# A decoder layer on one core: exponentials per PSUM bank, turned products alternating with scores, and the mixer's values in the ring banks

## The reference, cut to what matters

```python
x = x + mixer(layernorm(x))        # projection w1, depthwise conv, silu, running products
                                   # and sums over the tokens, C_w, D_w, gate w2, w3
x = x + attention(layernorm(x), ctx, ctx)
x = x + experts(layernorm(x))      # 8 experts, best 2, capacity 641, FF 1024
# attention: q from x; k, v from ctx; 16 heads of 16
scores = einsum('bhqd,bhkd->bhqk', q, k) * SCALE
scores = where(causal, scores, -inf)
probs = softmax(scores, axis=-1)
out = einsum('bhqk,bhkd->bhqd', probs, v) @ WO + bO
```

## Time and profile before

| | us |
|---|---|
| median of 3 runs (lowest to highest) | 697.65 (695.46 to 701.62) |
| the profiled execution's own time | 699.12 |
| its span, first to last instruction | 697.4 |
| mean granted clock of PE, as a share of 2.4 GHz | 0.926 |
| PE busy | 608.8 |

### The profile page before, as it was taken

How to read it: one execution, slowest core, us unless ns; L and a number is a source line. 1 busy time by engine, 2 the same in 40 slices (tenths; PEclk the granted TensorE clock), 3 DMA queues, 4 the chain that set the end, 5 groups by cost and what they waited for, 6 DMA issues and landing times.

```text
span 697.4 us, 11909 instructions
## 1 busy us (share of the span) xinstructions
PE 608.8 (87%) x4100; PEld 506.9 (73%) x4100; DVE 498.6 (71%) x1066; ACT 352.9 (51%) x685; POOL 334.2 (48%) x322
## 2 busy tenths in 40 slices
PE   3787998998989789899998725999999999999992
PEld 2666887787877545555564425999999999999991
DVE  6887687787688867678874442778787888788740
ACT  4774563663552333363534213566666666656551
POOL 1065324324340013331535464446776868686776
PEclk9897999999999989999987655999999999999997
DMA  8302306765338745955735006223626262621224
GB/s 281 119 31 43 109 31 160 258 180 150 92 93 226 170 112 139 240 147 155 191 117 184 23 15 199 99 86 91 163 41 179 27 178 30 172 32 14 26 33 45
DMA packets 63317, 81.65 MB, mean 117 GB/s; under 512 B 10296, under 2 KB 47939, under 8 KB 63257
## 3 DMA queue, kind: packets, MB, share of 16 engines
q1 hardware_dynamic: 53928, 72.85, 36.8%
q0 software_dynamic: 9216, 7.81, 7.8%
q10 hardware_dynamic: 112, 0.23, 0.1%
HBM read 48.27 MB, written 34.36 MB: 118 GB/s over the span
## 4 chain that ended last, share of the span: by engine, by line
PE 42%; DVE 5%; issue 4%; POOL 4%; DMA 4%; ACT 3%; ACTq 0%; SPq 0%; DVEq 0%; POOLq 0%
PE l_scores L101 13%; PE l_turned L1900 7%; PE l_out L1900 3%; PE l_shared L1900 3%; PE l_turned L340 2%; POOL out L1604 2%; ACT l_area L370 2%; PE l_scores L1834 2%; PE l_turned L324 2%; PE l_out L360 2%; PE l_shared L1776 2%; DMA l_q_more<-md 1%; PE l_scores L1857 1%; DMA l_hi<-md 1%; PE l_scores L265 1%
## 5 line engine op out<-in xcount | busy, mean ns | idle before, releaser
L2089 DVE SCALAR_TENSOR_TENSOR w_v<-w_th,l_scores 128x324 f32<-128x324 f32 x128 | 62.2, 490 | 55.0 <-ACT w_th L1691 53.7
L1691 ACT ACTIVATE w_th<-l_scores 128x324 f32<-128x324 f32 x128 | 56.4, 441 | 83.4 <-PE l_scores L101 82.1
L1591 POOL TENSOR_TENSOR l_lo<-w_v,l_hi 128x324 fp32r<-128x324 f32 x64 | 59.0, 922 | 74.6 <-ACT l_hi L1697 74.4
L370 ACT ACTIVATE l_area<-l_turned 128x1024 f32<-128x1024 f32 x48 | 49.1, 1023 | 82.4 <-PE l_turned L340 79.6
L101 PE MATMUL l_scores<-l_hi,w_w1h 128*128 128x324 f32 x256 | 81.0, 316 | 2.3 <-DVE l_lo L2081 1.2
L1604 POOL DMA_INDIRECT out<-l_area,w_to x48 | 76.3, 1591 | 12.0 <-issue 9.7
L101 PE MATMUL l_scores<-l_lo,w_w1h 128*128 128x324 f32 x256 | 80.3, 314 | 0.0
L101 PE MATMUL l_scores<-l_hi,w_w1l 128*128 128x324 f32 x256 | 80.1, 313 | 0.0
L294 DVE TENSOR_REDUCE l_nm<-l_scores 128x4 f32<-128x1024 f32 (+1 forms) x45 | 54.7, 1215 | 19.8 <-PE l_scores L280 19.6
L1697 ACT ACTIVATE l_hi<-w_v 128x324 fp32r<-128x324 f32 x128 | 59.9, 472 | 12.4 <-DVE w_v L2089 11.8
L2063 DVE TENSOR_TENSOR w_w2l<-w_s,w_w2h 128x256 fp32r<-128x256 f32 x56 | 60.9, 1088 | 1.9
(11 more groups left out here) (459 smaller groups left out, 1715.4 us busy)
## 6 DMA issues: line engine op xcount, KB each, us to landing
w_s<-in_L_ffn_w SPq DMA_DIRECT2D x14, 1024.0 KB, 7.4
disp<-c_blank SPq DMA_DIRECT2D x8, 658.1 KB
l_lo<-kd SPq DMA_DIRECT2D x26, 200.0 KB
l_hi<-qd SPq DMA_DIRECT2D x26, 192.0 KB
w_rows<-disp SPq DMA_DIRECT2D x7, 658.1 KB
kd<-l_qkh SPq DMA_DIRECT2D x16, 256.0 KB, 4.7
vd<-l_area SPq DMA_DIRECT2D x4, 1024.0 KB, 6.5
qd<-l_qkh SPq DMA_DIRECT2D x16, 256.0 KB, 4.2
```

The source lines that it names most:

```text
L370: act.activation(lead.pr[n % 3][:, :], lead.tbank[:, :], ACT.Exp, scale=SCALE).then_inc(A["exp"], 1)
L1591: pool.tensor_tensor(hl[:, g % 3, half(1)], v[:, n % 4, :], hh[:, g % 3, half(1)].bitcast(F32), ALU.subtract)\
L1691: act.activation(th[:, n % 2, :], hb[n % 2][:, 0:HALF], ACT.Tanh, scale=0.5).then_inc(F["th"], 1)
L2089: dve.scalar_tensor_tensor(v[:, n % 4, :], th[:, n % 2, :], 1.0, hb[n % 2][:, 0:HALF], ALU.add, ALU.mult).then_inc(F["v"], 1)
```

## The change

**Exponentials.** `exps` makes two ACT calls of 128x512, one per bank (e = 0, 1); `st` and `exp` are counted per bank, so every count that is compared with them doubles.

**Order of the products.** Where a step has both (t = 4 to 41), `turned_and_scores` takes the place of the separate parts: both masks of u; then for e = 0 and 1: the turned mask of that bank, which waits for the previous exponential of that bank alone, and the turned products of e alternating with the scores of 1 - e. Where one kind has four and the other two, the sequence is for example turned, score, score, turned, score, score. What the due steps put between turned products and scores (`ranks`) comes behind both.

**Mixer's values.** `V` leaves `PAIRS` (ten names, so each product keeps its pair in all blocks) and `values` writes ring banks 0 and 1. It waits for `ring` (chunk `A` 3 read) in place of `x_out` and `dx`; `mixed` waits for `x_out` and `dx` in place of `kl`; `turn_q` and `turn_x` wait for `kl` in place of `vf`; chunks `dl` 0 and `A` 0 of the next block wait for `vf`.

```diff
--- before.py
+++ after.py
@@ -164,7 +164,7 @@
 HIGH_ORDER = ("w1", "dl_w", "A_w", "B_w", "D_w", "WQ", "w2")
 LOW_VECTOR = ("w1", "dl_w", "A_w", "B_w", "D_w")
 LOW_GPSIMD = ("WQ", "w2")
-PAIRS = ("Q", "T", "D", "W1", "W2", "TC", "W3", "K", "V", "C", "TQ")
+PAIRS = ("Q", "T", "D", "W1", "W2", "TC", "W3", "K", "C", "TQ")
 LEAD = 6
@@ -212,7 +212,7 @@
 def lay(sp, A, M, lead, qd, kd, g):
     b, k = divmod(g, 2)
-    ge(sp, A["st"], 3 * (g - ITEMS + 1))
+    ge(sp, A["st"], 6 * (g - ITEMS + 1))
     if g == 0:
         sp.wait_ge(M["made"], 12 * NBLK)
         sp.wait_ge(M["D"], DC * NBLK)
@@ -266,19 +266,30 @@
                   start=True, stop=False, skip_group_check=True)
-def scores(pe, A, lead, u):
+def score(pe, lead, u, j, e):
+    g, s = divmod(u, 3)
+    p = j if s == 0 else 2 * s - 2 + j
+    rows, keys = slice(64 * e, 64 * e + 3 * HD), P if s == 0 else L
+    tok = slice(0, P) if s == 0 else slice(P, L)
+    at = e * 4 * P + j * keys
+    return pe.matmul(score_bank(lead, u)[:, at:at + keys], lead.q3[g % ITEMS][rows, p, tok],
+                     lead.k3[g % ITEMS][rows, p, 0:keys], start=False, stop=True, skip_group_check=True)
+def laid(pe, A, u):
     g, s = divmod(u, 3)
     if s == 0:
         pe.wait_ge(A[f"laid{g % ITEMS}"], LAID * (g // ITEMS + 1))
...
+def scores(pe, A, lead, u):
+    laid(pe, A, u)
+    for j in range(4 if u % 3 == 0 else 2):
+        for e in range(2):
+            mm = score(pe, lead, u, j, e)
     mm.then_inc(A["s"], 1)
@@ -307,46 +318,75 @@
     dve.transpose(lead.mt[g % 2][:, :], mx[:, :, :].rearrange("q n c -> q (n c)").bitcast(F32)).then_inc(A["mx"], 1)
...
+def turned_mask(pe, A, c, lead, n, e):
+    ge(pe, A["exp"], 2 * n + e - 1)
     if n == 0:
         pe.wait_ge(A["nm"], LEAD)
...
+    bank = lead.tbank[:, e * 4 * P:(e + 1) * 4 * P]
+    m = 4 if n % 3 == 2 else 2
+    out = bank.rearrange("k (p q) -> k p q", p=m)[:, :, 0:P]
+    pe.matmul(out, c["mask"][:, :], c["identb"][:, :].unsqueeze(1).to_broadcast([P, m, P]),
+              start=True, stop=False, skip_group_check=True)
+def turn_score(pe, lead, n, j, e):
+    g, s = divmod(n, 3)
+    p = j if s == 2 else 2 * s + j
+    rows = slice(64 * e, 64 * e + 3 * HD + 2)
+    tok = slice(P, L) if s == 2 else slice(0, L)
+    key = slice(P, L) if s == 2 else slice(0, P)
+    w = P if s == 2 else L
+    at = e * 4 * P + j * w
+    return pe.matmul(lead.tbank[:, at:at + w], lead.k3[g % ITEMS][rows, p, key], lead.q3[g % ITEMS][rows, p, tok],
+                     start=False, stop=True, skip_group_check=True)
+def maxima_in(pe, A, n):
     g, s = divmod(n, 3)
     if s == 0:
         pe.wait_ge(A[f"m_in{g % 2}"], 32 * (g // 2 + 1))
...
+def turned(pe, A, c, lead, n):
+    for e in range(2):
+        turned_mask(pe, A, c, lead, n, e)
+    maxima_in(pe, A, n)
+    count = 4 if n % 3 == 2 else 2
+    for j in range(count):
+        for e in range(2):
+            mm = turn_score(pe, lead, n, j, e)
+            if j == count - 1:
+                mm.then_inc(A["st"], 1)
+def turned_and_scores(pe, A, c, lead, t, u):
+    mask(pe, A, c, lead, u)
+    four_t, four_u = t % 3 == 2, u % 3 == 0
+    for e in range(2):
+        turned_mask(pe, A, c, lead, t, e)
+        if e == 0:
+            maxima_in(pe, A, t)
+            laid(pe, A, u)
+        for i in range(4):
+            if four_t or i % 2 == 0:
+                mt = turn_score(pe, lead, t, i if four_t else i // 2, e)
+                if i == (3 if four_t else 2):
+                    mt.then_inc(A["st"], 1)
+            if four_u or i % 2 == 0:
+                ms = score(pe, lead, u, i if four_u else i // 2, 1 - e)
+    ms.then_inc(A["s"], 1)
 def weigh(pe, A, lead, n):
     g, s = divmod(n, 3)
     b, k = divmod(g, 2)
-    pe.wait_ge(A["exp"], n + 1)
+    pe.wait_ge(A["exp"], 2 * n + 2)
     if s == 0:
         ge(pe, A["po"], 2 * g - 1)
         pe.wait_ge(A[f"v_in{b % 2}"], 16 * (b // 2 + 1))
@@ -365,9 +405,11 @@
 def exps(act, A, lead, n):
-    act.wait_ge(A["st"], n + 1)
     ge(act, A["pv"], n - 2)
-    act.activation(lead.pr[n % 3][:, :], lead.tbank[:, :], ACT.Exp, scale=SCALE).then_inc(A["exp"], 1)
+    for e in range(2):
+        act.wait_ge(A["st"], 2 * n + e + 1)
+        bank = slice(e * 4 * P, (e + 1) * 4 * P)
+        act.activation(lead.pr[n % 3][:, bank], lead.tbank[:, bank], ACT.Exp, scale=SCALE).then_inc(A["exp"], 1)
 def mixer_and_projections(nc, sems, c, lead, x_sb, bo, a, disp, qd, kd, vd, md):
@@ -851,7 +893,7 @@
                     if i == 0:
                         pe.wait_ge(S["ident"], 1)
                     ge(pe, S["xl2"], DC * (i - 2))
-                    ge(pe, S["vf"], 2 * (i - 1))
+                    ge(pe, S["kl"], DC * (i - 1))
                     turn([pair(i - 1, "T", k) for k in range(DC)], xn, "xT", ("xn", TPB * i))
                 def turn_c(i):
@@ -861,7 +903,7 @@
                     turn([pair(i, "TC", k) for k in range(DC)], cin, "cT")
                 def turn_q(i):
-                    pe.wait_ge(S["vf"], 2 * upto(i + 2))
+                    pe.wait_ge(S["kl"], DC * upto(i + 2))
                     turn([pair(i + 1, "TQ", k) for k in range(DC)], xn, "qT", ("xn2", TPB * i))
                 def products(name, m, xs):
@@ -882,6 +924,8 @@
                     if i == 0 and name == "B" and m == 0:
                         split_done(pe, "B_w")
                     ge(pe, S["ring"], made(i, name, m) - 4)
+                    if name in ("dl", "A") and m == 0:
+                        ge(pe, S["vf"], 2 * (i - 1) + (1 if name == "dl" else 2))
                     split_product(pe, ring(name, m)[:, :], products(name + "_w", m, (sh, sl))).then_inc(S["made"], 1)
                 def first_chunks():
@@ -914,7 +958,8 @@
                 def mixed(i, m):
                     pe.wait_ge(S["gh"], HC * (i + 1))
                     pe.wait_ge(S["gl"], HC * (i + 1))
-                    pe.wait_ge(S["kl"], DC * (i + 1))
+                    pe.wait_ge(S["dx"], DC * (i + 1))
+                    ge(pe, S["x_out"], 2 * i)
                     split_product(pe, pair(i, "C", m)[:, :], products("C_w", m, (gh, gl))).then_inc(S["C"], 1)
                 def w2(i):
@@ -923,9 +968,7 @@
                     pe.wait_ge(S["ssmh"], DC * (i + 1))
                     pe.wait_ge(S["ssml"], DC * (i + 1))
                     pe.wait_ge(S["dx"], DC * upto(i + 2))
-                    if i == NBLK - 1:
-                        pe.wait_ge(S["vf"], 2 * NBLK)
-                    else:
+                    if i < NBLK - 1:
                         ge(pe, S["ql"], DC * i)
                     for m in range(DC):
                         split_product(pe, pair(i + 1, "W2", m)[:, :], products("w2", m, late_input(i))).then_inc(S["w2"], 1)
@@ -962,12 +1005,11 @@
                         split_product(pe, pair(i, "K", m)[:, :], products("WK", m, (xbh, xbl))).then_inc(S["k"], 1)
                 def values(i):
-                    ge(pe, S["x_out"], 2 * i)
-                    pe.wait_ge(S["dx"], DC * (i + 1))
+                    pe.wait_ge(S["ring"], made(i, "A", 3))
                     for n in range(2):
                         for j in range(2):
                             tok = slice((2 * n + j) * P, (2 * n + j + 1) * P)
-                            mm = split_product(pe, pair(i, "V", n)[:, j * D:(j + 1) * D],
+                            mm = split_product(pe, banks[n][:, j * D:(j + 1) * D],
                                                [((xbh[:, k, tok], xbl[:, k, tok]), weights("WV", k, 0, D)) for k in range(DC)])
                         mm.then_inc(S["v"], 1)
@@ -982,14 +1024,14 @@
                 def unit(u):
                     if u == 0:
                         pe.wait_ge(S["ring"], 12 * NBLK)
+                        pe.wait_ge(S["vf"], 2 * NBLK)
                     if u == 1:
                         pe.wait_ge(S["hs"], DC * NBLK)
                     mask(pe, A, c, lead, u)
                     scores(pe, A, lead, u)
                 def step(t):
-                    turned_mask(pe, A, c, lead, t)
-                    turned(pe, A, lead, t)
+                    turned(pe, A, c, lead, t)
                 turn_x(0)
                 w1(0)
@@ -1209,7 +1251,7 @@
                         dve.wait_ge(S["vzero"], 1)
                     ge(dve, S["v_st"], 16 * i)
                     for s in range(2):
-                        ins = dve.tensor_tensor(v_rows(n, s), v_heads(pair(i, "V", n), s), v_heads(bv, s), ALU.add)
+                        ins = dve.tensor_tensor(v_rows(n, s), v_heads(banks[n], s), v_heads(bv, s), ALU.add)
                     ins.then_inc(S["vf"], 1)
                 dve.wait_ge(S["x0"], 16)
@@ -1904,17 +1946,13 @@
                 for t in range(START, END):
                     u = t + LEAD
-                    if t < NS:
-                        turned_mask(pe, A, c, lead, t)
                     if u < NS:
-                        mask(pe, A, c, lead, u)
-                    if t < NS:
-                        turned(pe, A, lead, t)
```

(20 more changed lines are left out.)

18 lines of the change are left out of this document (removed).

## The result

The changed kernel is slower. The forecast was 702.0 with a range of 689 to 710, so it is missed, upwards. The profiled execution took 715.32 us (span 713.6), 16.2 more than the one before.

The account below looks back on a forecast made before the run. PE was taken to bound mixer and attention. Profiled 699.1 plus attention 10.0 (13.5 - 6.6 + 3.1) less mixer 5.6 gave 703.5, or 702.0 us against the median; range 689 to 710, the forecast's own range 696 to 707.

Parts of the forecast that it names:

- The step that failed: Bound of mixer and attention: PE sets the time, so its work and stalls count; clock 0.95 read, no term given.
- three signs: Would refute the forecast: step with s = 1 at 1.9 us or less, lone products 0.2 apart, mixer under 3 us earlier.
- The longer steps: Attention: added PE work, less stalls removed, plus longer waits for the maxima, +10.0 us in sum.
- The passage: Attention, 38 steps: one more switch between full-height masks and half-height products, 0.29 us a step.
- The lone products: Attention, 25 steps with s = 0 or 2: unpaired half-height products take whole places, net 0.10 us a step.
- The third rival: Attention: a lone product can't load its weights ahead, 11 us on top, 713; chance 0.09.
- The stalls: Attention: 21 steps where the turned mask waits 0.31 us on average for the exponential; all go, -6.6 us.
- The maxima's way: Attention: maxima's transfers get 0.62 us less time, five groups without slack, +3.1 us.
- The mixer: Mixer blocks: values no longer wait for the residual, until DVE is late next; -5.6 us, between -2.5 and -7.5.
- The second: Attention: the maxima's transfers set the period and light groups wait 1.5 to 2 us, 708; chance 0.13.
- the first: Attention: alternation nearly free, passages 0.09 us a step, no tighter maxima transfers; -8.8 us, about 689; chance 0.22.
- the fourth: Mixer: none of the gain arrives because DVE's chain is the bound, 707.6; chance 0.08.

Follow-up runs that it names:

- passage_in_pairs: no_alternation with the scores' masks moved from ahead of the turned products to behind them, so a mask stands mid-step without alternation; 708.35 us, 1.018 of before.
- double_masks: Changed kernel with each turned mask multiplied twice in steps 4 to 41; 723.37 us, 1.037 of before.
- halved_middle: Changed kernel with the turned mask in the middle of the step at half height, leaving out half the tokens' mask in one bank; 707.24 us.
- mask_blocks: Changed kernel with the first turned mask repeated 8 more times in step 5 and 16 more in steps 22 and 34; 719.13 us.
- mixer_only: Kernel before with only the mixer's part of the change; 692.25 us against 696.3, ratio 0.995.
- no_alternation: Changed kernel with all turned products ahead of the scores again, in pairs of both halves, two exponential calls and mixer kept; 690.18 us against 696.3, ratio 0.994.
- masks_first: Changed kernel with both turned masks ahead of both halves of the alternating products, so no mask mid-step; 694.76 us, 1.001 of before.
- double_masks_pairs: no_alternation with each turned mask multiplied twice in steps 4 to 41; 694.61 us.
- one_call: no_alternation with one call of the exponential in place of two; 693.04 us against 698.1, ratio 0.9945.
- loads_between: no_alternation with the two loads of the maxima issued between the two exponential calls instead of behind both; 701.19 us, 1.005 of before.
- changed_again: The changed kernel unaltered, measured and profiled a second time; 720.84 us.
- att_only: Changed kernel with the mixer of before, so the attention's part of the change alone; 719.91 us, 23.6 over before.

## Why the prediction was wrong

**The step that failed** is the one that is not in the sum: it was made at full clock, though the rows that it began with already showed 0.95 in the attention. "PE sets the time in both, so what counts is what PE must do and where it stands still" leaves out at which clock it does it. That term measured +14.1 us in the profile (43.3 us at half in place of 9.8, by 0.42), and more in the second one. It also gives the scatter, from 708.26 us at a mean clock of 0.927 to 730.94 at 0.894, four runs in that order: from these clocks the fastest spent some 103 us at half and the slowest 155, and 0.42 of the difference is 22 us, where the times differ by 22.7.

What the runs show of its cause: long stretches (17 to 31 us) are in all seven profiles of the six kernels that have a mask between a step's half-height products (changed, twice, attention alone, passage_in_pairs, double_masks, halved_middle, mask_blocks); in the seven without it (before, mixer_only, no_alternation, masks_first, double_masks_pairs, one_call, loads_between) none is over 10.2 in the 38 steps:

| kernel | mask in the middle | 38 steps, us | at half | longest stretch | less 0.42 x half |
|---|---|---|---|---|---|
| before | no | 109.9 | 9.8 | 6.8 | 105.8 |
| mixer_only | no | 110.9 | 13.4 | 10.2 | 105.2 |
| no_alternation | no | 106.6 | 9.5 | 6.8 | 102.6 |
| masks_first | no | 109.0 | 12.4 | 6.8 | 103.8 |
| one_call | no | 109.7 | 15.9 | 6.8 | 103.1 |
| double_masks_pairs | no | 110.2 | 5.3 | 3.4 | 108.0 |
| loads_between | no | 116.8 | 26.6 | 10.2 | 105.6 |
| changed | yes | 131.9 | 43.3 | 27.3 | 113.7 |
| changed_again | yes | 141.2 | 66.4 | 27.3 | 113.3 |
| att_only | yes | 123.8 | 25.8 | 20.5 | 112.9 |
| passage_in_pairs | yes | 127.2 | 47.0 | 27.3 | 107.5 |
| double_masks | yes | 144.5 | 52.6 | 30.7 | 122.4 |
| halved_middle | yes | 127.7 | 64.5 | 23.9 | 100.6 |
| mask_blocks | yes | 137.2 | 43.6 | 23.9 | 118.9 |

Taking the mask out of the middle saves 25 us with the alternation, putting it in costs 18 without. Excluded are the mixer's shift (1), the two calls (3), the alternation (4, 5), the step's length (8) and the drain at the change of height in the middle (9). What it is about the mask's place that lets the clock stay at half, and why it falls at all at these places while PE is busy, stays open.

**The longer steps were priced nearly right.** 113.7 - 105.8 = 7.9 us at full clock, forecast 10.0. None of the three signs came by which the forecast would have known itself wrong (a step with s = 1 of 1.9 us or less, lone products 0.2 apart, a mixer less than 3 us earlier): none of them looked at the clock.
- The passage: s = 1 takes 2.08 against 1.79 without it, 0.29 to 0.30, forecast 0.29. That holds in every second light step; in the others no_alternation waits for DVE's transpose and takes 2.06, so against it the passage costs next to nothing. Before and in the changed kernel `weigh` of units 12, 18 and 30 also starts only 0.10 to 0.14 behind that transpose's end: DVE is late next there. Steps that had no stall to lose show passage and lone products together, forecast 0.39: 3.19 for 2.79 in step 20, 4.97 for 4.54 in step 23.
- The lone products: s = 2 takes 2.61 in the changed kernel and 2.46 in passage_in_pairs, so 0.15, forecast 0.10; without the passage they cost 0.01, with s = 0 0.05 (masks_first against no_alternation). The third rival falls, and with it the rule quoted from the Trainium skill ("TensorE: Matmul & The Clock Gate", Part 3) for this kernel: products of one half follow at 0.11 to 0.12 there too.
- The stalls: 2.17 + 0.29 - 2.08 = 0.38 in a step with s = 1, forecast 0.31, and the wait of the turned mask for ACT is gone from the list. But the reason was half wrong: one_call shows that for s = 1 the scores' masks, put first, hide the whole exponential, where I had given the credit to the second call.
- The maxima's way: the load is issued at 300.53, 1.62 us into the step that starts at 298.91, forecast 1.6. Counted as how late each group's first turned product is in its step, the waits are 3.5 us against 2.5 before, +1.0 in place of +3.1. Three groups ran at half clock there and waited for nothing; that this is the reason is not shown. In the list of waits the matmuls have 3.1 us for 2.2. With it the sum at full clock is 13.5 - 6.6 + 1.0 = 7.9. That this meets the measured 7.9 is luck in part: the lone products cost more than forecast and the stalls gave more (38 x 0.29 + 25 x 0.15 - 21 x 0.38 = 6.8, forecast 6.9). The lists of waits of the changed kernel, 253.3 to 386.3, of the weight loads and of the matmuls:

```profile
PEld l_turned L342 <- DMA l_hi<-md: 5.0, 5, 1.7
```

```profile
PE l_turned L342 <- DMA l_hi<-md: 3.1, 3, 1.3
```

and of the matmuls before, 258.2 to 368.8:

```profile
PE l_turned L340 <- DMA l_q_more<-md: 1.4, 2, 1.0
...
PE l_turned L340 <- DMA l_hi<-md: 0.8, 2, 0.5
```

**The mixer held**, with -4.9 of the -5.6: `queries` of block 2 at 119.34 (forecast 120), PE idle there for 1.1 us by the row, 1.5 from start to start (119.34 - 117.83), forecast 1.4. mixer_only has -4.4 in the profile and -4 in the medians.

**The rivals.** None of them is what happened. The second (maxima, 708) and the third (lone products, 713) gave higher times for reasons that the profile denies; the first, that passages are nearly free, falls with the 0.20 of the timeline; the fourth falls with the mixer. After the mixer (-4.4 at step 3's `weigh`) and the steps (+7.9) the rest of the kernel gives back 1.4, and +2.1 would have been the change of the profiled time without the clock: 701.2, near the forecast's 703.5 for that execution and inside its own range. That is an estimate; no run has the changed order at the clock of before.

## What to carry to other kernels

Read the clock's column as a term of the sum: for each stretch the time at half, and a step's length at half and at full clock, before any edit is priced. Where a hand-written order keeps full-height products together, an order that scatters them is to be timed for its clock and not by its distances; here the clock took 14 us in the profile where the longer steps took 8. Of this change keep the mixer's part (mixer_only, 0.995 of before). The scores' masks put first shorten the 38 steps by 2.1 us at full clock (one_call, 103.1 for 105.2), but its time, 0.9945 of before, and 0.9943 with the second call, is not told apart from the mixer's part alone. And leave the queue of the exponentials free of anything that waits for a transfer.

## What was not expected of the hardware

- The clock stayed at half for 27.3 us while PE was busy 27.30 of them. The Trainium skill, "TensorE: Matmul & The Clock Gate", Part 1, has the clock follow how busy PE has been; the trace doesn't agree where busy is the profile's busy time.
- At half clock PE reads 100% busy, and its steps are 1.7 to 1.8 times as long (3.54 for 2.08, 4.61 for 2.61, 8.32 for 4.54 in a step with a projection).
- The clock fell while PE read busy without a gap: 18.10 of 18.10 us ahead of the fall at 363.30.
- In the kernels with a mask in the middle all 15 stretches of 17 us or more ended in or right behind step 9, 15, 27 or 39 of the 48, which hold a projection's products, and none of them had passed such a step before. That these products bring the clock back is not shown.
- From a full-height mask's start to that of a half-height product 0.20 us pass, and as long the other way; from a half-height mask to its own product 0.03.
- A pair of DMA issues between two calls on ACT costs 0.2 to 0.4 us of ACT, even where nothing is waited for.
